# One largest logit for two pairs of graphs, and zero products in two gaps, in a four-layer graph network

## The reference

```
# layers 0 and 1 (attention)
h = x @ W.T;  e = leaky_relu(h@a_src [rows] + h@a_dst [columns], 0.2)
alpha = softmax(where(adj == 0, -big, e));  y = alpha @ h
# layer 2
alpha = sigmoid(where(adj == 1, leaky_relu((h * a0) @ h.T), -big))   # adj 2..4 likewise with a1..a3
y = alpha @ h + bias
# layer 3
y = sum_r (adj == r) @ x @ weight[r-1] + bias
# after each layer
x = layernorm(x + y)
```

## Time and profile before

| what | value |
|---|---|
| median of 3 runs | 245.51 us (245.35 to 246.8) |
| profiled execution | 246.51 us |
| its span, first to last instruction | 244.7 us |
| mean granted TensorE clock | 0.963 |

### The profile page before, as it was taken

One profiled execution on the slowest core, in us unless ns is written; L12 is line 12 of the kernel. 1 busy time (PEld: TensorE's weight loads), 2 busy tenths in 40 slices (PEclk: granted clock), 3 DMA queues, 4 the chain that ended last, 5 costly groups with the idle time before them and its releaser, 6 DMA issues.

```text
span 244.7 us, 5718 instructions
## 1 busy us (share of the span) xinstructions
PE 225.0 (92%) x1749; PEld 207.1 (85%) x1749; DVE 223.4 (91%) x747; ACT 188.3 (77%) x603; POOL 172.9 (71%) x262
## 2 busy tenths in 40 slices
PE   7689999999999999999999999999999999989730
PEld 7589899888999998989999998999998988868620
DVE  1838999899999999999999999999999999999980
ACT  2257879788779899899576869958699899778670
POOL 5002516995698789776677978878599988887870
PEclk9959999999999999999999999999999999999955
DMA  7970962433047023002720040004001011000034
GB/s 182 238 244 4 206 184 43 93 126 43 4 136 161 7 87 44 1 0 47 233 83 30 3 129 1 4 1 129 3 0 47 0 44 46 0 0 3 3 129 135
DMA packets 12145, 17.57 MB, mean 72 GB/s; under 512 B 1104, under 2 KB 5968, under 8 KB 12112
## 3 DMA queue, kind: packets, MB, share of 16 engines
q1 hardware_dynamic: 9520, 12.85, 15.8%
q0 software_dynamic: 2304, 4.20, 10.5%
q10 hardware_dynamic: 288, 0.14, 0.2%
HBM read 17.17 MB, written 4.19 MB: 87 GB/s over the span
## 4 chain that ended last, share of the span: by engine, by line
PE 56%; DVE 32%; issue 4%; DMA 2%; POOL 1%; ACT 1%; DVEq 0%
PE banks L1176 25%; PE banks L1115 9%; DVE wgt_all L856 7%; DVE fstats L909 6%; PE banks L1143 6%; DVE fres_all L901 5%; PE banks L1100 4%; PE banks L1133 3%; DVE fres_all L889 3%; PE banks L1173 3%; DVE banks L819 3%; DMA xT_all<-x_turned 2%; DVE wgt_all L864 2%; PE banks L1153 2%; PE banks L1184 1%
## 5 line engine op out<-in xcount | busy, mean ns | idle before, releaser
L540 POOL TENSOR_TENSOR frstd<-fvar,minus_half 128x4 f32<-128x4 f32 x64 | 64.9, 1021 | 17.4 <-DVE fvar L915 6.0
L1176 PE MATMUL banks<-vals_all,wgt_all 128*128 128x129 f32 x512 | 64.3, 280 | 0.6 <-issue 0.6
L1176 PEld LDWEIGHTS banks<-vals_all,wgt_all 128*128 128x128 f32 x512 | 61.3, 196 | 1.5 <-issue 1.0
L856 DVE SCALAR_TENSOR_TENSOR wgt_all<-banks,gain,mask_all 128x256 f32<-128x256 f32 x128 | 52.6, 469 | 0.0
L909 DVE BATCH_NORM_STATS2 fstats<-fres_all 128x6 f32<-128x256 f32 x128 | 47.4, 414 | 0.1
L535 POOL TENSOR_TENSOR xb_all<-xs_all,bias_cen 128x256 f32<-128x256 f32 x60 | 42.3, 728 | 1.1 <-ACT xs_all L684 1.0
L684 ACT ACTIVATE xs_all<-fres_all,frstd 128x128 f32<-128x128 f32 x116 | 37.2, 404 | 2.3 <-POOL frstd L540 2.3
L1176 PE MATMUL banks<-xs_all,wgt_all 128*128 128x128 f32 x256 | 31.8, 277 | 0.5 <-DVE wgt_all L864 0.5
L1176 PEld LDWEIGHTS banks<-xs_all,wgt_all 128*128 128x128 f32 x256 | 29.8, 192 | 1.6 <-DVE wgt_all L864 1.5
L1143 PE MATMUL banks<-fxT,fxTa 128*128 128x256 f32 x128 | 30.4, 381 | 0.3 <-issue 0.3
L611 ACT COPY fxT<-banks 128x256 f32<-128x256 f32 x64 | 20.7, 386 | 7.8 <-PE banks L1100 7.5
(11 more groups left out here) (93 smaller groups left out, 409.0 us busy)
## 6 DMA issues: line engine op xcount, KB each, us to landing
xT_all<-x_turned SPq DMA_DIRECT2D x16, 256.0 KB, 3.7
mask_all<-adj_turned POOLq DMA_DIRECT2D x16, 256.0 KB, 5.2
x_all<-x_laid SPq DMA_DIRECT2D x16, 256.0 KB, 3.9
out<-xs_all SPq DMA_DIRECT2D x16, 256.0 KB, 2.2
bias<-biases_laid SPq DMA_DIRECT2D x1, 128.0 KB, 6.3
w_pack<-W_and_columns ACTq DMA_DIRECT2D x1, 68.0 KB, 2.9
w_fast<-W_turned ACTq DMA_DIRECT2D x1, 64.0 KB, 3.2
w_nat<-in_L_gnn_W SPq DMA_DIRECT2D x1, 64.0 KB, 5.1
```

The source lines that it names most:

```text
L540: nc.gpsimd.tensor_tensor(frstd[:, int(l), slot(n), :], fvar[:, int(l), slot(n), :], minus_half[:, :, :], ALU.pow).then_inc(fast_pool[k], 1)
L856: last = nc.vector.scalar_tensor_tensor(out=wgt(u)[:, c, :], in0=place(f"rows{l}", u), scalar=gain[:, u, c, 1:2], in1=maskT(u)[:, c, :], o ...
L1176: last = nc.tensor.matmul(place(f"out{l}", u)[:, b * width:(b + 1) * width], wgt(u)[:, c, b * P:(b + 1) * P], (vals if l in "01" else xs)( ...
```

## The change

Three things are changed.

- Pairs of graphs are grouped for `dT`, `peak`, `top` and `dmax`. The second pair of a group, its leader, does the four steps for both: `dT` turns the logits of two pairs (128x8 into 8x128), `peak` works on eight rows, `top` spreads eight numbers, `dmax` takes the largest of eight. `v` of both pairs uses the leader's number, and so waits for the leader's `dmax`. A softmax isn't changed by the number that is taken off, so the output is the same. Groups follow from which `dT` steps the list has. Layer 0 has `dT` of 0, 1, 3, 5, 7, 9, 11, 13, 15. Layer 1 has it of 0, 1, 3, 5, 7, 9, 11, 13, 14, 15.
- Two `warm` steps are in TensorE's list: `warm:3` ahead of `rows0:0`, and `warm:4` ahead of `h0:3`.
- All five lists and the bank table are new. Some small steps change engines. The counts of steps (a step is a pair) that changed:

The diff of the functions, and the starts of the lists (the rest of the lists is new in the same way):

```diff
+def leader(l, n):
+    return next(m for m in sorted(m for name, layer, m in order("pe") if name + layer == f"dT{l}") if m >= n)
+def members(l, n):
+    return [m for m in range(n + 1) if leader(l, m) == n]
...
-        top = sb("top", [H * NB, TEAMS])
+        top = sb("top", [2 * H * NB, TEAMS])
...
             def exponentials(l, n, k):
-                act.wait_ge(fast_dve[k], at("dve", f"dmax{l}", n * H))
+                led = leader(l, n)
+                act.wait_ge(fast_dve[led % K], at("dve", f"dmax{l}", led * H))
...
-                nc.scalar.activation(vals_all[:, pair(n, VALS), :, D], logit[:, int(l), slot(n), :, 1], ACT.Exp, bias=minus_dmax[:, n:n + 1]).then_inc(fast_act[k], 1)
+                nc.scalar.activation(vals_all[:, pair(n, VALS), :, D], logit[:, int(l), slot(n), :, 1], ACT.Exp, bias=minus_dmax[:, led:led + 1]).then_inc(fast_act[k], 1)
...
             def peak(l, n, k):
                 dve.wait_ge(fast_pe[k], at("pe", f"dT{l}", n * H))
-                nc.vector.tensor_reduce(top[:, n:n + 1], place(f"h{l}", n * H)[0:H * NB, 260:260 + P], AX.X, ALU.max).then_inc(fast_dve[k], 1)
+                rows = len(members(l, n)) * H * NB
+                nc.vector.tensor_reduce(top[0:rows, n:n + 1], place(f"h{l}", n * H)[0:rows, 260:260 + P], AX.X, ALU.max).then_inc(fast_dve[k], 1)
...
             def gather_d(l, n, k):
-                copier = doer(f"logits{l}", n)
-                pe.wait_ge(signals[copier][k], at(copier, f"logits{l}", n * H))
+                led = members(l, n)
+                for m in led:
+                    copier = doer(f"logits{l}", m)
+                    pe.wait_ge(signals[copier][m % K], at(copier, f"logits{l}", m * H))
...
 sp
-xT:1 xT:0 weights:0 xT:2 weights:1 xT:4 weights:2 xT:3 x:0 x:2 x:1
+xT:1 xT:0 weights:0 weights:1 xT:4 weights:2 xT:2 xT:3 x:1 x:5 x:3 x:0 x:2
 pe
-h0:0 h0:1 rows0:0 dT0:1 turn:0 dT0:0 rows0:1 top0:1 top0:0 h0:2 dT0:2 h0:4 out0:0 dT0:4 top0:2 rows0:2 out0:1
+h0:1 h0:0 rows0:1 dT0:1 turn:0 top0:1 dT0:0 warm:3 rows0:0 top0:0 out0:1 warm:4 h0:3 h0:2 dT0:3 h0:4 top0:3 rows0:3 rows0:4 rows0:2 out0:0
 act
-gains0:0 logits0:1 gains0:1 logits0:2 gains0:2 v0:0 vals0:0 logits0:4 v0:1 vals0:1 seen:2
+logits0:1 gains0:1 logits0:0 seen:1 v0:1 gains0:0 vals0:1 v0:0 seen:2 seen:3 vals0:0 logits0:2 logits0:3
 dve
-logits0:0 centre:0 weight0:0 peak0:0 peak0:1 weight0:1 centre:1 dmax0:0 centre:2 dmax0:1 peak0:2 centre:3
+centre:0 peak0:1 weight0:1 dmax0:1 peak0:0 centre:2 dmax0:0 centre:1 weight0:0 rsum0:1 centre:3 rinv0:1 peak0:3 res0:1 dmax0:3 stats0:1 weight0:3
 pool
-mask:0 mask:1 mask:2 mask:5 mask:4 mask:7 var0:0
+mask:1 mask:2 mask:0 mask:3 mask:7 mask:4 mask:6 mask:5 mask:10 mask:8 pow0:1
 BANKS
-    "h0": "01 23 47 45 56 30 27 67 34 25 56 13 01 34 01 23",
-    "rows0": "4 6 3 3 6 7 5 0 0 7 0 4 6 5 4 0",
+    "h0": "23 01 47 56 23 05 74 56 05 34 67 01 13 70 56 73",
+    "rows0": "4 4 5 0 1 3 6 0 6 7 7 6 0 3 2 4",
```

More of the change, by code:

```diff
@@ L837, in peak @@
                 dve.wait_ge(fast_pe[k], at("pe", f"dT{l}", n * H))
-                nc.vector.tensor_reduce(top[:, n:n + 1], place(f"h{l}", n * H)[0:H * NB, 260:260 + P], AX.X, ALU.max).then_inc(fast_dve[k], 1)
+                rows = len(members(l, n)) * H * NB
+                nc.vector.tensor_reduce(top[0:rows, n:n + 1], place(f"h{l}", n * H)[0:rows, 260:260 + P], AX.X, ALU.max).then_inc(fast_dve[k], 1)
             def largest(l, n, k):
                 dve.wait_ge(fast_pe[k], at("pe", f"top{l}", n * H))
-                nc.vector.tensor_reduce(minus_dmax[:, n:n + 1], place(f"h{l}", n * H)[:, 400:400 + H * NB], AX.X, ALU.max, negate=True).then_inc(fast_dve[k], 1)
+                nc.vector.tensor_reduce(minus_dmax[:, n:n + 1], place(f"h{l}", n * H)[:, 400:400 + len(members(l, n)) * H * NB], AX.X, ALU.max, negate=True).then_inc(fast_dve[k], 1)
             def scales(l, n, k):
@@ L1119, in gather_d @@
             def gather_d(l, n, k):
-                copier = doer(f"logits{l}", n)
-                pe.wait_ge(signals[copier][k], at(copier, f"logits{l}", n * H))
-                nc.tensor.transpose(place(f"h{l}", n * H)[0:H * NB, 260:260 + P], logit[:, int(l), slot(n), :, 1].rearrange("p u b -> p (u b)"), ident[:, :]).then_inc(fast_pe[k], 1)
+                led = members(l, n)
+                for m in led:
+                    copier = doer(f"logits{l}", m)
+                    pe.wait_ge(signals[copier][m % K], at(copier, f"logits{l}", m * H))
+                dst_logits = logit[:, int(l), led[0] * H:(n + 1) * H, :, 1].rearrange("p u b -> p (u b)")
+                nc.tensor.transpose(place(f"h{l}", n * H)[0:len(led) * H * NB, 260:260 + P], dst_logits, ident[:, :]).then_inc(fast_pe[k], 1)
             def spread_top(l, n, k):
                 pe.wait_ge(fast_dve[k], at("dve", f"peak{l}", n * H))
-                nc.tensor.transpose(place(f"h{l}", n * H)[:, 400:400 + H * NB], top[:, n:n + 1].to_broadcast([H * NB, P]), ident[0:H * NB, 0:H * NB]).then_inc(fast_pe[k], 1)
+                rows = len(members(l, n)) * H * NB
+                nc.tensor.transpose(place(f"h{l}", n * H)[:, 400:400 + rows], top[0:rows, n:n + 1].to_broadcast([rows, P]), ident[0:rows, 0:rows]).then_inc(fast_pe[k], 1)
             def spread_rows(l, n, k):
```

## The result

The changed kernel took 242.22 us in the median of 4 runs (241.19 to 243.26), the kernel before 245.43 us (244.52 to 246.8). The ratio is 0.9884, with a 95% interval of 0.9845 to 0.9922. On another chip it took 242.0 us beside 245.08 us, a ratio of 0.9874 (0.9825 to 0.9923). So the change saves 1.2%, about 3 us. The profiled execution took 242.28 us with a span of 240.2 us, 4.5 us less than that of before; 1 us of this is that the profiled execution of before was a long one. The medians are over all executions; the ratios leave out the few that were over 1.5% above the fastest of their kernel.

A forecast was written before the change was run, and what follows sets the result against it. TensorE and VectorE were taken as both full, with no single bound. Removed -3.4, head -0.3, waits +1.2, rest 0 gave -2.5 us; with 1.0 for the long profiled execution and 0.3 for the lists' freedom, 242.7 us, range 239.6 to 247.0.

The forecast's parts named there:

- the prediction's own signs: Wrong if both engines shrink 3.4 us each and the span doesn't follow, or the tail moves over 1.5 us.
- the tail: Kernel's end, from 200 us on: a chain of latencies; 0 taken, bounds -1.5 and +1.5 us.
- Removed work: Body: 13 each of `dT`, `peak`, `top`, `dmax` go, 3.4 us less on TensorE and on VectorE; -3.4 us.
- Waits added: TensorE waiting for `h` banks or values, held longer by grouped pairs: +1.2 us, bounds 0 and 7.8.
- cases 3 and 4: Body waits: 3, saving eaten, near 245.5 us (chance 0.25); 4, slower, 248.6 us (0.13).
- Rival 4: Body: `h` banks held for two pairs are the bound; 3.1 us slower, 248.6 us; chance 0.13.
- Head: Kernel's start: gain of 0.3 us, between 1.6 gained if the clock stays up and 1.1 lost if it falls.
- Steps that change engine: Small steps moved among VectorE, ScalarE and GpSimd: VectorE's net 0; 0 us taken, bounds -1 and +1.

The follow-up runs named there:

- every pair alone: The changed kernel with the 13 first pairs' own `dT`, `peak`, `top` and `dmax` put back: 244.48 us, 0.9974 of the kernel before.
- `out1:0` ahead: The changed kernel with `out1:0` ahead of `h1:3`, `h0:5` ahead of `dT1:3`, and three VectorE steps ahead of `logits1:3`: 244.83 us, 0.9989 of the kernel before.
- the new head: The changed kernel with `rows0:0` in bank 7, `dmax0:1` before `weight0:1`, `h0:2` before `h0:3`, four zero products before `rows0:0` only: 240.11 us, 0.981.

## Why the prediction came out

The time was right, 242.7 forecast and 242.2 measured, the range held it, and the sign was right. Its terms were not, and they cancelled: that the sum met the time to 0.5 us is luck. By the prediction's own signs two things went wrong. The span didn't follow the 3.4 us that it took from both engines, and the tail moved by more than 1.5 us.

- *Removed work, -3.4.* The spacing of the single steps was right: in the trace of before, the median time from start to start is 0.15 us for `top`, 0.11 for `dT`, 0.20 for `peak` and 0.07 for `dmax`, and the wide ones after are at 0.15, 0.11, 0.20 and 0.08. The conversion was not. Measured by putting it back: 1.7 us in the body. A likely reason is that the gaps of two full engines lie at different places, and a step taken out of one beside the other's full stretch only widens a gap; no experiment shows this. The further 1.0 us that it gives came from the length of TensorE's program, which the prediction didn't have.
- *Waits added, +1.2.* Too low, and put down to the wrong thing. The lists lost 2.5 us between 32 and 49 us. Where the waits stood was named rightly, but with every pair alone they were there as well: the order of the steps was the cause. The sign that cases 3 and 4 asked for, over 3 us of TensorE's idle time put down to `vals`, didn't come: it is 0.7 us in the whole profile. Rival 4's mechanism is real, as the experiment with `out1:0` ahead shows, but the changed kernel only touches it.
- *Head, -0.3.* +0.6 in the two profiles, which is within what one kernel's profiles scatter. The timed executions say more. If body and end take in them what they take in the profiles (206.9 and 5.5 us before, 203.7 and 3.65 after), their median spans on one chip, 243.3 and 240.0 us, leave 30.9 us for the head before and 32.6 after: an estimate of +1.7, and the same working gives +1.8 for two other versions with this head. So this term, and not the waits, took back most of what the tail and the branch gave beyond the forecast. The start of the zeros (10.9, measured 10.97), the length of `out0:1` (3.4, 3.18) and the fall of the clock were right. The idle time ahead of the zeros was not (over 2 us, measured 1.35), nor was the start of `out0:1` (12.0, measured 12.84), nor the next `h`, put behind 18 us with a falling clock (16.76). That the clock falls where it did is no constant: that varies by 2 us from execution to execution, and sometimes it doesn't fall. All five profiles with an early rise fell at 11.3 to 11.8 us, zeros or not. Of the nine with a late rise, one of the six with zeros ahead of `rows0:0` fell in the head, and both of the new lists without them did; the old lists' one didn't.
- *Steps that change engine, 0, and the tail, 0.* These failed, and they are further off than any other term: between 211 us and the flag the changed kernel gains 3.0 us, outside of both terms' bounds. Putting seven of the steps back costs 3.1 us from 32 us to the flag in the profile, 1.0 of it at the fallen clock, and 1.3 to 1.6 us in the timed executions, most of it in the tail. The prediction added up VectorE's work and found it even; it should have asked which step stands ahead of the last `res` and `low`. In the other lists the same move loses, so it is no constant of its own; it goes with the order.
- *Not in the prediction at all:* 1.9 us of the profiled difference behind the flag, the branch.

What the new order gives by itself between 125 and 167 us (2.3 us, of which putting the removed work back takes 0.5) was only seen, not tested: no experiment undoes the order of the body alone.

## What to carry to other kernels

When two engines are full, the work taken from both is not the gain. Here it was half of it; look in the trace for which steps it frees. Follow a change by the time at which equal work is done, not by busy shares: here it showed that a kernel that ends 4.5 us earlier was still behind at 211 us. Where the body is as rigid as this, compare from a point behind the head: one profile says nothing sure of a head whose clock rises at 5 us in one execution and at 9 in the next. And with orders written by hand, a delay of a step that frees a bank can come through nearly in full, and the fallen clock can nearly double it (1.9 and 1.6 us with `out1:0` ahead), so a local repair must be followed one round further, over the engine that waits for the bank.

## What the runs showed of the hardware

- TensorE's branch past code that isn't run took 0.35 or 0.36 us in nine profiles of the changed kernel and its versions, 3.07 us in the version with each pair alone, and 3.80 us in the one that is 56 instructions longer; in the three profiles with the lists of before it took 3.77, 3.77 and 4.19 us.
- The same program's TensorE clock rose at 5.0 us in one execution and at 10.2 in another (the changed kernel's two profiles), and the first `h` took 2.02 and 3.81 us. The mean granted clock of the two is nearly the same (0.979 and 0.981); it doesn't count the time ahead of its record.
- The granted clock fell to 0.50 (1.2 GHz) at 42.8 us, in the middle of a dense body (`out1:0` ahead), after TensorE had waited 0.44, 0.32, 0.28, 0.37 and 1.53 us between 32 and 41.6 us, and it was still there from 44 to 46 us, with TensorE fully busy. With nearly the same five waits it fell at 41.3 us in the version without `warm:4`. In the changed kernel waits of 0.45, 0.37 and 0.78 us at that place brought no fall. The Trainium skill, page "TensorE: Matmul & The Clock Gate", section "HAM oscillation — how this bites in real kernels", describes such falls behind much longer waits for transfers, and this one isn't of that kind; it is nearer to the section "A second HAM failure mode: psum-queue depth-cycling", which has the clock fall where TensorE idles shortly but often. This trace agrees with that one as far as its five waits go; the section gives no length of such an idle time to hold them against. (The prediction says that the page doesn't lead one to expect a fall with TensorE only partly idle; that holds for the section named there, not for this one.)
- Where zero products filled TensorE's wait in the head, the mean granted clock of the executions was higher, in both pairs of versions that differ in them alone (0.9805 to 0.991 with the changed head on one chip, 0.982 to 0.990 with the new head on two). In the old lists the clock came back sooner in the profile, but over the timed executions its mean stayed as it was (0.982 and 0.982). `warm:4`, which filled no wait, took 0.9 us of TensorE, and no gain of it is seen.
